# Layer 3 reads its bf16 high part in place; VectorE normalises the next tile ahead of the second row's gated products

## The chip, the cores and the metric

One core of a Trainium2 chip runs the whole kernel as one launch. The metric is the device time of one execution in microseconds; the figure shown is the median of three runs. The engines are PE (TensorE; PEld is its weight load), DVE (VectorE), ACT (ScalarE), POOL (GpSimd) and SP, which issues the DMAs.

## The reference

Four layers work on one image x of 192 by 192 pixels with 64 channels, each as `x = x + L(group_norm(x))`. Cut to what matters, with i, j, k pixel indices and d a channel:

```python
# layers 0, 1, 2
xn = layernorm(v)                               # over the 64 channels, v = group_norm(x)
left, right = (xn@Wl)*sigmoid(xn@Wlg), (xn@Wr)*sigmoid(xn@Wrg)   # times a mask in layers 0 and 1
out = einsum('bikd,bjkd->bijd', left, right)    # layer 2: 'bkjd,bkid->bijd', divided by 192
x = x + (layernorm(out) * sigmoid(xn@Wog)) @ Wout     # layer 1 gates after Wout
# layer 3: no layernorm ahead of the projections
left, right = (v@Wl)*sigmoid(v@Wlg)*mask, (v@Wr)*sigmoid(v@Wrg)*mask
x = x + (layernorm(einsum('bkjd,bkid->bijd', left, right)) @ W_out) * sigmoid(v@W_gate)
```

Layer 0 rounds left and right to bf16 before the einsum; the others are float32.

## The kernel before

The 128 partitions hold 64 channels of two image halves. A tile is two image rows of both halves, 128 by 384 values; each layer has 48 tiles (TILES), and each tile has two rows r = 0, 1, so there are 96 row steps (SUBS) per layer. A layer is three phases in turn: **phase_a** (input normalisation, gate, projections, the products left and right kept in `lr`), **phase_b1** (the einsum, channel by channel) and **phase_b2** (output normalisation, output matmul, residual). The change touches phase_a alone. No planner is at work: every engine has its own queue, written out by hand, and runs strictly in that order; counters (semaphores) hold an instruction until what it needs is there. `over_tiles` calls an engine's `step(n, ...)` for n = 0 to 47, with buffers that rotate by n.

How a tile goes through phase_a of **layers 0, 1 and 2** (`ln` is true):

- PE `centre` (L466) subtracts the channel mean; ACT `centred` copies it out (L715) and squares it (L717); DVE `square_low` (L957) takes the low part of the square; PE `variance` (L474) sums; DVE `var_eps` (L962) copies the variance out; POOL raises it to -1/2 (L1153) and widens it (L1160); PE `spread` (L483) transposes that into PSUM bank 2; DVE `normalise` (L972) multiplies it with the centred tile, which gives `xn`.
- ACT `high` (L748) writes xn + 1 to `val`: float32 in layer 0, and in layers 1 and 2 its bf16 rounding, the high part. There DVE `low` (L978) writes the rest as a second bf16 tile, the low part. Layers 1, 2 and 3 multiply in three passes: high data by high weights, high data by low weights, low data by high weights. Layer 0 has one float32 pass.
- PE `gate` (L493) makes the output gate's argument. PE `project` makes those of one row's left and right: `wide` (L511) 128 of the row's 192 pixels, `narrow` (L521) the other 64. Here the data tile is the weight that is loaded, and the weight matrix streams.
- ACT `sigmoids` (L739) takes one row's gates out of PSUM. DVE `glu` (L989, four instructions for a row, in layers 0, 1 and 3; L996, one instruction, in layer 2) multiplies them with the values in PSUM, writes `lr`, and raises `a_free`: this row's PSUM banks are free.

In **layer 3** there is no layer norm: ACT `plain` (L724) makes xn from the loaded tile, ACT `high` rounds it to bf16, DVE `low` takes the rest. centre, variance, spread, var_eps and normalise don't exist there.

The orders in one step n, which the prediction rests on:

- PE: gate(n), spread(n+1), project(n, 0), project(n, 1), centre(n+4), variance(n+3).
- ACT, layers 0 to 2: gate(n), high(n+1), sigmoids(n, 0), sigmoids(n, 1), centred(n+4). Layer 3: gate(n), high(n+1), plain(n+2), sigmoids(n, 0), sigmoids(n, 1).
- DVE: glu(n-1, 1), var_eps(n+2), normalise(n+1), square_low(n+3), low(n+1), glu(n, 0); in layer 3 only glu(n-1, 1), low(n+1), glu(n, 0).
- SP: the load of a later tile, then the store of gate n to DRAM.

The waits that tie them: `normalise(n+1)` waits for spread(n+1) (`a_bc`), `gate(n)` on PE for low(n) (`a_lo`; layer 0: for high(n)). `project(n, 0)` waits for glu(n-1, 0) ahead of its first pass, and in the layers with a norm ahead of the last pass of `wide` for glu(n-1, 1) as well:

```python
if r == 0 or not ln:
    pe.wait_ge(a_free, l * SUBS + m + 1)         # m = 2n + r; a_free starts at 2
...
if ln and r == 0 and stop:                       # stop: the last of the passes
    pe.wait_ge(a_free, l * SUBS + m + 2)
```

With one pass (layer 0) that is ahead of all of `wide`. In layer 3 project(n, 1) waits for glu(n-1, 1) itself.

Of the kernel before, what the change touches and what calls it, by code (L numbers as in the profile page):

```python
# [20 lines left out]
BF16 = mybir.dt.bfloat16  # L21
U8 = mybir.dt.uint8
ALU = mybir.AluOpType
ACT = mybir.ActivationFunctionType
# [5 lines left out]
ROWS = 2  # L30
# [4 lines left out]
RING = 4  # L35
# [4 lines left out]
SUBS = ROWS * TILES  # L40
# [20 lines left out]
def build_triangle_layers(nc, x_in, params, consts, mask3_k, mask3_row, x_out):  # L61
# [5 lines left out]
    with ExitStack() as ctx:  # L67
        def sb(name, shape, dt=F32):
            return ctx.enter_context(nc.sbuf_tensor(name, shape, dt))

        def sem(name):
            return ctx.enter_context(nc.semaphore(name))

        def sems(name, n=RING):
# [12 lines left out]
        xn = sb("xn", [P, 2, TILE])  # L87
# [33 lines left out]


        sq_high = sq[:, :, :].bitcast(BF16).rearrange("p s (f e) -> p s f e", e=2)[:, :, :, 1]

        xn_parts = val[:, :, :].bitcast(BF16).rearrange("p s (a f) -> p s a f", a=2)

# [28 lines left out]
        a_z, a_cen, a_sq, a_var, a_ve, a_rstd, a_rb, a_bc, a_xn = (  # L155
            sem("a_" + s) for s in ("z", "cen", "sq", "var", "ve", "rstd", "rb", "bc", "xn"))
        a_hi, a_lo, a_sq_lo = sem("a_hi"), sem("a_lo"), sem("a_sq_lo")
        a_gate_mm, a_gate, a_proj, a_sig, a_free = (
            sem("a_" + s) for s in ("gate_mm", "gate", "proj", "sig", "free"))
# [92 lines left out]
        def parts_before(l):  # L252
            return sum(TILES for m in range(l) if IN_PARTS[m])

        def slot_free(eng, semaphore, value):

            if not (isinstance(value, int) and value <= 0):
                eng.wait_ge(semaphore, value)
# [158 lines left out]
        def _(pe):  # L417
# [19 lines left out]
            def phase_a(l):  # L437
                base = l * TILES
                ln = HAS_LN[l]
# [5 lines left out]
                passes = ((0, 0), (1, 0), (0, 1)) if IN_PARTS[l] else ((0, 0),)  # L445

                def moving(part, s):
                    return xn_parts[:, s % 2, part, :] if IN_PARTS[l] else val[:, s % 2, :]

                def half(h):  # L450
# [251 lines left out]
        def _(act):  # L702
            def phase_a(l):
                base = l * TILES
                ln = HAS_LN[l]
                act.wait_ge(gn_dve, 7 * (l + 1))
                act.wait_ge(params_ready, l + 1)

                def centred(n, s):


                    act.wait_ge(a_z, base + n + 1)
                    slot_free(act, a_xn, base + n - RING + 1)
                    slot_free(act, a_var, base + n - 1)
                    nc.scalar.activation(cen[:, s, :], ps[:, s % 2, 0:TILE], ACT.Identity, bias=gn_cb)\  # L715
                        .then_inc(a_cen, 1)
                    nc.scalar.activation(sq[:, s % 2, :], ps[:, s % 2, 0:TILE], ACT.Square, bias=gn_cb)\  # L717
                        .then_inc(a_sq, 1)

                def plain(n, i, s):  # L720

                    act.wait_ge(in_loaded[s], in_count(l) + 16 * (i + 1))
                    slot_free(act, a_lo, parts_before(l) + n - 1)
                    nc.scalar.activation(xn[:, s % 2, :], in_ring[:, s, :], ACT.Identity, bias=gn_b, scale=gn_a)\  # L724
                        .then_inc(a_xn, 1)

                def gate(n, i, s):
                    act.wait_ge(a_gate_mm, base + n + 1)

                    slot_free(act, gate_stored[s], 16 * (l * TURNS + i))  # L730
                    nc.scalar.activation(gate_ring[:, s, :], ps[:, 3, 0:TILE], ACT.Sigmoid, bias=gate_bias[:, 0:1])\  # L731
                        .then_inc(a_gate, 1)

                def sigmoids(n, s, r):
                    m = ROWS * n + r
                    act.wait_ge(a_proj, l * SUBS + m + 1)

                    act.wait_ge(a_free, l * SUBS + m + 1)
                    nc.scalar.activation(act_out[:, r, :].rearrange("p (h c) -> p h c", h=2),  # L739
                                         ps[:, 4 + 2 * r:6 + 2 * r, COLS:2 * COLS], ACT.Sigmoid).then_inc(a_sig, 1)  # L740

                def high(n, s):


                    act.wait_ge(a_xn, base + n + 1)
                    slot_free(act, a_proj, l * SUBS + ROWS * (n - 1))
                    out = xn_parts[:, s % 2, 0, :] if IN_PARTS[l] else val[:, s % 2, :]
                    nc.scalar.activation(out, xn[:, s % 2, :], ACT.Copy, bias=1.0 if ln else 0.0).then_inc(a_hi, 1)  # L748

                def step(n, i, s, ahead):  # L750
                    gate(n, i, s)
                    if not ln and ahead >= 1:
                        high(n + 1, (s + 1) % RING)
                    if not ln and ahead >= 2:
                        plain(n + 2, i + (s + 2) // RING, (s + 2) % RING)
                    if ln and ahead >= 1:
                        high(n + 1, (s + 1) % RING)
                    sigmoids(n, s, 0)
                    sigmoids(n, s, 1)
                    if ln and ahead >= 4:  # L760
                        centred(n + 4, s)

                if ln:
                    centred(0, 0)
                    centred(1, 1)
                    centred(2, 2)
                    centred(3, 3)
                    high(0, 0)
                else:
                    plain(0, 0, 0)  # L770
                    high(0, 0)
                    plain(1, 0, 1)
                over_tiles(act, step)

# [90 lines left out]
        def _(dve):  # L865
# [77 lines left out]
            def phase_a(l):  # L943
                base = l * TILES
                ln = HAS_LN[l]
# [19 lines left out]
                def normalise(n, s):  # L965
                    dve.wait_ge(a_bc, base + n + 1)
                    dve.wait_ge(a_cen, base + n + 1)
                    if IN_PARTS[l]:
                        slot_free(dve, a_lo, parts_before(l) + n - 1)
                    else:  # L970
                        slot_free(dve, a_hi, base + n - 1)
                    nc.vector.tensor_tensor(xn[:, s % 2, :], ps[:, 2, 0:TILE], cen[:, s, :], ALU.mult)\  # L972
                        .then_inc(a_xn, 1)

                def low(n, s):

                    dve.wait_ge(a_hi, base + n + 1)
                    nc.vector.scalar_tensor_tensor(xn_parts[:, s % 2, 1, :], xn[:, s % 2, :], 1.0 if ln else 0.0,  # L978
                                                   xn_parts[:, s % 2, 0, :], ALU.add, ALU.subtract).then_inc(a_lo, 1)

                def glu(n, r):
                    m = ROWS * n + r
                    dve.wait_ge(a_sig, l * SUBS + m + 1)
                    sig = act_out[:, r, :].rearrange("p (h c) -> p h c", h=2)
                    if HAS_MASK[l]:

                        for h in range(2):
                            for t, (lo, hi) in enumerate(((0, P), (P, COLS))):
                                ins = nc.vector.scalar_tensor_tensor(  # L989
                                    out5[:, h, lo // 2:hi // 2, :, m],  # L990
                                    ps[:, 4 + 2 * r + h, lo:hi].rearrange("p (a e) -> p a e", e=2),
                                    mask4[:, t, h, bass.ds(m, 1)],
                                    sig[:, h, lo:hi].rearrange("p (a e) -> p a e", e=2), ALU.mult, ALU.mult)
                        ins.then_inc(a_free, 1)
                    else:
                        nc.vector.tensor_tensor(  # L996
                            out5[:, :, :, :, m],
                            ps[:, 4 + 2 * r:6 + 2 * r, 0:COLS].rearrange("p h (a e) -> p h a e", e=2),
                            sig.rearrange("p h (a e) -> p h a e", e=2), ALU.mult).then_inc(a_free, 1)

                def step(n, i, s, ahead):
                    if not (isinstance(n, int) and n == 0):
                        glu(n - 1, 1)
                    if ln and ahead >= 2:
                        var_eps(n + 2, (s + 2) % RING)
                    if ln and ahead >= 1:
                        normalise(n + 1, (s + 1) % RING)
                    if ln and ahead >= 3:
                        square_low(n + 3, (s + 3) % RING)
                    if IN_PARTS[l] and ahead >= 1:  # L1010
                        low(n + 1, (s + 1) % RING)
                    glu(n, 0)
# [107 lines left out]
            for q in range(PIECES):  # L1120
                dve.wait_ge(x_loaded[q], 16)
                with dve.Fori(q * TURNS // PIECES, (q + 1) * TURNS // PIECES) as i:
                    for s in range(RING):
                        n = i * RING + s
# [183 lines left out]
```

## Time and profile before

| | |
|---|---|
| median of 3 runs | 1529.07 us (1520.78 to 1530.68) |
| profiled execution: its own time, span | 1531.67 us, 1529.5 us |
| busy share of the span: PE, DVE, ACT, POOL | 84%, 68%, 63%, 36% |
| mean granted TensorE clock | 0.948 of full speed |
| busiest DVE group: L989, the gated products | 276.3 us busy, 61.7 us idle before, 55.6 of it until ACT L739 |
| phase_a, first to last tile: layers 0, 1, 2, 3 | 186.7, 172.6, 160.0, 130.7 us |

The shares are averages over twelve phases with different limits, so they do not say what one phase waits for. In a timeline row the bracket names the idle time of that engine just before the row and what ended it. Matmuls are pipelined: the time from one row's start to the next one's start is what the engine spent on it, and the duration reaches to the modelled end of its last result.

### The profile page before, as it was taken

What the parts mean: (1) busy time and instruction counts of PE and PEld (TensorE: products, weight loads), DVE (VectorE), ACT (ScalarE), POOL (GpSimd) and SP (SyncE); (2) the same over time, 40 slices, a digit from 0 to 9 for tenths busy, and PEclk for the clock granted to TensorE, in tenths of its full rate; (3) what the DMA queues carried; (4) which work ended last, traced back from release to release, by engine and by line L of the source; (5) the groups of instructions that cost most, each with busy time, mean ns of one, the idle gap of its engine ahead of it and who ended that gap; (6) DMA issues with size and microseconds to landing.
All of it is one profiled execution on the core that took longest, in us unless ns stands there. A gap on an engine that the chain in (4) does not pass through costs nothing. (4 is left out here: it accounts for less than half of the span.)

```text
span 1529.5 us, 43851 instructions
## 1 busy us (share of the span) xinstructions
PE 1282.1 (84%) x12950; PEld 765.9 (50%) x12950; DVE 1041.8 (68%) x2976; ACT 962.0 (63%) x2093; POOL 543.4 (36%) x490
## 2 busy tenths in 40 slices
PE   0899998787789998989941999999789677799898
PEld 0455554444345455755521666667455333367455
DVE  7577774299789996219950788831499788821587
ACT  0577774489577774129940888831599688822575
POOL 0455551055456563005530666610156200000355
PEclk9899999899899999999975899999899899999999
DMA  8011113467533332896667333359689444369798
GB/s 275 27 52 46 51 51 111 114 202 225 169 101 103 106 115 72 254 286 177 195 152 188 103 115 113 108 174 300 180 262 278 154 141 138 129 185 307 212 291 258
DMA packets 206501, 249.31 MB, mean 163 GB/s; under 512 B 29024, under 2 KB 196320, under 8 KB 206432
## 3 DMA queue, kind: packets, MB, share of 16 engines
q1 hardware_dynamic: 206432, 248.42, 53.1%
q8 instruction: 40, 0.66, 0.2%
q14 instruction: 29, 0.24, 0.0%
HBM read 139.83 MB, written 108.53 MB: 162 GB/s over the span
## 5 line engine op out<-in xcount | busy, mean ns | idle before, releaser
L989 DVE SCALAR_TENSOR_TENSOR lr<-ps,mask,act_out 128x128 f32 (+5 forms) x1152 | 276.3, 310 | 61.7 <-ACT act_out L739 55.6
L1153 POOL TENSOR_TENSOR rstd<-ve,half_col 128x6 f32<-128x6 f32 x144 | 190.2, 1321 | 259.1 <-DVE ve L962 225.4
L511 PE MATMUL ps<-w_parts,val 64*128 64x256 bf16 (+1 forms) x2112 | 222.6, 304 | 47.4 <-DVE lr L989 41.9
L1196 POOL TENSOR_TENSOR new_ring<-val,lr 128x384 f32<-128x384 f32 x96 | 103.4, 1078 | 409.5 <-issue 325.0
L1186 POOL TENSOR_TENSOR val<-act_out,gate_ring 128x384 f32<-128x384 f32 x96 | 118.4, 1233 | 247.2 <-ACT act_out L817 231.1
L739 ACT ACTIVATE act_out<-ps 128x384 f32<-128x384 f32 x384 | 174.9, 481 | 34.2 <-PE ps L511 16.7
L783 ACT ACTIVATE in_ring<-ps 128x768 f32<-128x768 f32 (+1 forms) x64 | 51.8, 810 | 184.0 <-PE ps L579 161.9
L511 PEld LDWEIGHTS ps<-w_parts,val 64*128 64x128 bf16 (+1 forms) x2112 | 90.5, 111 | 133.3 <-DVE lr L989 94.7
L1085 DVE TENSOR_TENSOR sq_low<-sq 128x384 bf16<-128x384 f32 x192 | 120.1, 625 | 52.9 <-ACT sq L796 52.8
L621 PE MATMUL ps<-in_ring,k 128*128 128x384 f32 x288 | 134.5, 555 | 20.1 <-DMA in_ring<-t_scratch 19.7
L715 ACT ACTIVATE cen<-ps,gn 128x384 f32<-128x384 f32 x144 | 83.6, 581 | 104.1 <-PE ps L466 101.5
L794 ACT ACTIVATE cen<-ps 128x384 f32<-128x384 f32 x192 | 104.5, 544 | 66.9 <-PE ps L621 66.4
L748 ACT ACTIVATE val<-xn 128x384 bf16<-128x384 f32 (+1 forms) x192 | 99.9, 521 | 64.1 <-PE ps L521 41.1
L579 PE MATMUL ps<-lr 64*128 64x192 f32 (+3 forms) x896 | 129.2, 335 | 12.8 <-DVE lr L989 5.2
L1036 DVE COPY cen<-ps 128x384 f32<-128x384 f32 x48 | 26.7, 557 | 162.1 <-PE ps L579 158.4
L1160 POOL TENSOR_TENSOR rb<-rstd,one_col 128x384 f32<-128x384 f32 x144 | 129.0, 896 | 11.3
L466 PE MATMUL ps<-in_ring,w_centre 128*128 128x192 f32 (+1 forms) x288 | 93.6, 440 | 44.4 <-issue 44.2
L579 PEld LDWEIGHTS ps<-lr 64*128 64x128 f32 (+3 forms) x896 | 105.5, 181 | 33.6 <-issue 18.4
L809 ACT ACTIVATE rb<-rstd 128x384 f32<-128x384 f32 x192 | 110.4, 575 | 17.6 <-DVE rstd L1046 17.1
L731 ACT ACTIVATE gate_ring<-ps,gate_bias 128x384 f32<-128x384 f32 x192 | 111.5, 581 | 12.6 <-PE ps L493 8.3
L521 PE MATMUL ps<-w_parts,val 64*64 64x128 bf16 (+1 forms) x4224 | 119.0, 234 | 0.0
L957 DVE TENSOR_TENSOR sq_low<-sq 128x384 bf16<-128x384 f32 x144 | 79.8, 554 | 55.6 <-ACT sq L717 55.6
(101 smaller groups left out, 2574.8 us busy)
## 6 DMA issues: line engine op xcount, KB each, us to landing
gate_scratch<-gate_ring SPq DMA_DIRECT2D x192, 192.0 KB, 2.2
gate_ring<-gate_scratch SPq DMA_DIRECT2D x96, 384.0 KB, 3.7
in_ring<-x_scratch SPq DMA_DIRECT2D x144, 192.0 KB, 2.4
lr<-x_scratch SPq DMA_DIRECT2D x72, 384.0 KB, 4.5
in_ring<-t_scratch SPq DMA_DIRECT2D x144, 192.0 KB, 3.3
x_scratch<-new_ring SPq DMA_DIRECT2D x48, 384.0 KB, 2.9
t_scratch<-in_ring SPq DMA_DIRECT2D x48, 384.0 KB, 3.4
lr<-x SPq DMA_DIRECT2D x6, 1536.0 KB, 15.3
```

Of the source, the lines that this page charges most:

```text
L511: mm = nc.tensor.matmul(banks[h][:, :, 0:P], moving(x, s)[half(h), N * r:N * r + P], proj_weights(w, h)[:, 0:2 * P], start=start, stop=sto ...
L521: mm = nc.tensor.matmul(banks[h][TAIL * e:TAIL * e + TAIL, :, P:COLS], moving(x, s)[half(h), N * r + P:N * r + N], proj_weights(w, h)[:, 2 ...
L579: mm = nc.tensor.matmul(ps[:, b + i % 2, N * (i // 2):N * (i // 2) + N], left[:, 0:P], right, start=first and i < 2, stop=last and i >= 2, ...
L621: nc.tensor.matmul(ps[:, s % 2, 0:TILE], w_c, t_slots(l, s)[:, 0, :], start=True, stop=True).then_inc(b2_z, 1)
L731: nc.scalar.activation(gate_ring[:, s, :], ps[:, 3, 0:TILE], ACT.Sigmoid, bias=gate_bias[:, 0:1])\
L739: nc.scalar.activation(act_out[:, r, :].rearrange("p (h c) -> p h c", h=2), ps[:, 4 + 2 * r:6 + 2 * r, COLS:2 * COLS], ACT.Sigmoid).then_i ...
L809: nc.scalar.activation(rb[:, s % 2, :].rearrange("p (a c) -> p a c", c=C), rstd[:, s % 2, :].rearrange("p (a o) -> p a o", o=1) .broadcast ...
L989: ins = nc.vector.scalar_tensor_tensor(out5[:, h, lo // 2:hi // 2, :, m], ps[:, 4 + 2 * r + h, lo:hi].rearrange("p (a e) -> p a e", e=2), ...
L1085: nc.vector.tensor_tensor(sq_low[:, s % 2, :], sq[:, s % 2, :], sq_high[:, s % 2, :], ALU.subtract).then_inc(b2_sq_lo, 1)
L1153: nc.gpsimd.tensor_tensor(rstd[:, s % 2, :], ve[:, s % 2, :], half_col[:, :], ALU.pow)\
L1160: nc.gpsimd.tensor_tensor(rb[:, s % 2, :].rearrange("p (a c) -> p a c", c=C), rstd[:, s % 2, :].rearrange("p (a o) -> p a o", o=1) .broadc ...
L1186: nc.gpsimd.tensor_tensor(val[:, s % 2, :], act_out[:, s % 2, :], gate_ring[:, s, :], ALU.mult)\
```

## The change

`xn_high` is a view of the float32 tile `xn` that takes the upper two bytes of each value: a bf16 number, cut off and not rounded, at every second bf16 position. Layer 3's PE reads it where it read the high part in `val`, ACT's `high` goes in layer 3, and DVE's `low` subtracts the view from xn with another instruction. `low` now waits for xn itself, and for the PE to be done with the tile before last; `plain`, whose tile PE now reads too, waits for PE where it waited for `low`, and stands behind the sigmoids in ACT's step. In layers 0, 1 and 2 DVE's `glu(n-1, 1)` stands behind `var_eps(n+2)` and `normalise(n+1)`, where it stood ahead of them.

```diff
--- before.py
+++ after.py
@@ -122,6 +122,8 @@
 
         sq_high = sq[:, :, :].bitcast(BF16).rearrange("p s (f e) -> p s f e", e=2)[:, :, :, 1]
 
+        xn_high = xn[:, :, :].bitcast(BF16).rearrange("p s (f e) -> p s f e", e=2)[:, :, :, 1]
+
         xn_parts = val[:, :, :].bitcast(BF16).rearrange("p s (a f) -> p s a f", a=2)
 
         w_whole = w_parts[:, :, :].rearrange("p a f -> p (a f)").bitcast(F32)
@@ -445,6 +447,8 @@
                 passes = ((0, 0), (1, 0), (0, 1)) if IN_PARTS[l] else ((0, 0),)
 
                 def moving(part, s):
+                    if not ln and part == 0:
+                        return xn_high[:, s % 2, :]
                     return xn_parts[:, s % 2, part, :] if IN_PARTS[l] else val[:, s % 2, :]
 
                 def half(h):
@@ -720,7 +724,7 @@
                 def plain(n, i, s):
 
                     act.wait_ge(in_loaded[s], in_count(l) + 16 * (i + 1))
-                    slot_free(act, a_lo, parts_before(l) + n - 1)
+                    slot_free(act, a_proj, l * SUBS + ROWS * (n - 1))
                     nc.scalar.activation(xn[:, s % 2, :], in_ring[:, s, :], ACT.Identity, bias=gn_b, scale=gn_a)\
                         .then_inc(a_xn, 1)
 
@@ -745,20 +749,18 @@
                     act.wait_ge(a_xn, base + n + 1)
                     slot_free(act, a_proj, l * SUBS + ROWS * (n - 1))
                     out = xn_parts[:, s % 2, 0, :] if IN_PARTS[l] else val[:, s % 2, :]
-                    nc.scalar.activation(out, xn[:, s % 2, :], ACT.Copy, bias=1.0 if ln else 0.0).then_inc(a_hi, 1)
+                    nc.scalar.activation(out, xn[:, s % 2, :], ACT.Copy, bias=1.0).then_inc(a_hi, 1)
 
                 def step(n, i, s, ahead):
                     gate(n, i, s)
-                    if not ln and ahead >= 1:
-                        high(n + 1, (s + 1) % RING)
-                    if not ln and ahead >= 2:
-                        plain(n + 2, i + (s + 2) // RING, (s + 2) % RING)
                     if ln and ahead >= 1:
                         high(n + 1, (s + 1) % RING)
                     sigmoids(n, s, 0)
                     sigmoids(n, s, 1)
                     if ln and ahead >= 4:
                         centred(n + 4, s)
+                    if not ln and ahead >= 2:
+                        plain(n + 2, i + (s + 2) // RING, (s + 2) % RING)
 
                 if ln:
                     centred(0, 0)
@@ -768,7 +770,6 @@
                     high(0, 0)
                 else:
                     plain(0, 0, 0)
-                    high(0, 0)
                     plain(1, 0, 1)
                 over_tiles(act, step)
 
@@ -974,9 +975,15 @@
 
                 def low(n, s):
 
-                    dve.wait_ge(a_hi, base + n + 1)
-                    nc.vector.scalar_tensor_tensor(xn_parts[:, s % 2, 1, :], xn[:, s % 2, :], 1.0 if ln else 0.0,
-                                                   xn_parts[:, s % 2, 0, :], ALU.add, ALU.subtract).then_inc(a_lo, 1)
+                    if ln:
+                        dve.wait_ge(a_hi, base + n + 1)
+                        nc.vector.scalar_tensor_tensor(xn_parts[:, s % 2, 1, :], xn[:, s % 2, :], 1.0,
+                                                       xn_parts[:, s % 2, 0, :], ALU.add, ALU.subtract).then_inc(a_lo, 1)
+                    else:
+                        dve.wait_ge(a_xn, base + n + 1)
+                        slot_free(dve, a_proj, l * SUBS + ROWS * (n - 1))
+                        nc.vector.tensor_tensor(xn_parts[:, s % 2, 1, :], xn[:, s % 2, :], xn_high[:, s % 2, :],
+                                                ALU.subtract).then_inc(a_lo, 1)
 
                 def glu(n, r):
                     m = ROWS * n + r
@@ -999,12 +1006,12 @@
                             sig.rearrange("p h (a e) -> p h a e", e=2), ALU.mult).then_inc(a_free, 1)
 
                 def step(n, i, s, ahead):
-                    if not (isinstance(n, int) and n == 0):
-                        glu(n - 1, 1)
                     if ln and ahead >= 2:
                         var_eps(n + 2, (s + 2) % RING)
                     if ln and ahead >= 1:
                         normalise(n + 1, (s + 1) % RING)
+                    if not (isinstance(n, int) and n == 0):
+                        glu(n - 1, 1)
                     if ln and ahead >= 3:
                         square_low(n + 3, (s + 3) % RING)
                     if IN_PARTS[l] and ahead >= 1:
```

## Rows read from the trace of the kernel before

**Rows 1.** Windows: start:end, length, busy us of PE, PEld, DVE, ACT, POOL, clock, DMA.

```profile
51.30:238.00 186.70, 183.28 (x1703) 104.31 (x1703) 138.97 (x507) 136.62 (x276) 99.81 (x94) 0.98 0.14 49
...
420.90:593.50 172.60, 155.53 (x2306) 85.59 (x2306) 159.66 (x555) 130.10 (x277) 101.85 (x93) 0.99 0.31 100
...
1207.10:1337.80 130.70, 100.81 (x1776) 47.62 (x1776) 109.16 (x406) 114.23 (x231) 0.00 (x0) 0.98 0.42 136
```

**Rows 2.** One line in layers 0, 1, 2, 3: ns min/median/max, first to last start.

```profile
L972 DVE TENSOR_TENSOR xn<-ps,cen x48: 545/557/558, 51.3 to 238.0; 128x384 f32<-128x384 f32 x48
...
L972 DVE TENSOR_TENSOR xn<-ps,cen x48: 541/545/558, 420.9 to 593.5; 128x384 f32<-128x384 f32 x48
...
L972 DVE TENSOR_TENSOR xn<-ps,cen x48: 556/558/559, 843.1 to 1003.1; 128x384 f32<-128x384 f32 x48
...
L724 ACT ACTIVATE xn<-in_ring,gn x48: 692/695/706, 1207.1 to 1337.8; 128x384 f32<-128x384 f32 x48
```

**Rows 3.** Timeline of layer 0: start, us, engine, line, op, [idle before <-releaser].

```profile
150.85 0.99 DVE L989 SCALAR_TENSOR_TENSOR lr<-ps,mask,act_out 128x128 f32 x4 [0.17 <-issue]
...
151.86 0.56 DVE L972 TENSOR_TENSOR xn<-ps,cen 128x384 f32<-128x384 f32 x1
...
151.90 0.70 PE L511 MATMUL ps<-w_parts,val 64*128 64x256 f32 x4
...
155.39 0.49 PE L483 MATMUL ps<-k,rb 128*128 128x128 f32 x3
...
155.92 0.56 DVE L972 TENSOR_TENSOR xn<-ps,cen 128x384 f32<-128x384 f32 x1 [0.23 <-PE ps L483]
```

**Rows 4.** Timeline of layer 1.

```profile
501.93 0.55 DVE L972 TENSOR_TENSOR xn<-ps,cen 128x384 f32<-128x384 f32 x1
...
502.00 0.28 PE L511 MATMUL ps<-w_parts,val 64*128 64x256 bf16 x2 [0.30 <-DVE lr L989]
...
502.22 0.53 PE L521 MATMUL ps<-w_parts,val 64*64 64x128 bf16 x24
...
502.40 0.55 DVE L957 TENSOR_TENSOR sq_low<-sq 128x384 bf16<-128x384 f32 x1
...
504.50 0.51 PE L483 MATMUL ps<-k,rb 128*128 128x128 f32 x3
```

**Rows 5.** Timeline of layer 2.

```profile
855.16 0.53 PE L521 MATMUL ps<-w_parts,val 64*64 64x128 bf16 x24
...
856.46 1.01 DVE L996 TENSOR_TENSOR lr<-ps,act_out 128x384 f32<-128x384 f32 x2
...
857.45 0.49 PE L483 MATMUL ps<-k,rb 128*128 128x128 f32 x3
```

**Rows 6.** Timeline of layer 3.

```profile
1281.19 0.36 PE L521 MATMUL ps<-w_parts,val 64*64 64x128 bf16 x12
...
1282.20 0.98 ACT L739 ACTIVATE act_out<-ps 128x384 f32<-128x384 f32 x2
...
1282.85 1.89 DVE L989 SCALAR_TENSOR_TENSOR lr<-ps,mask,act_out 128x128 f32 x8 [0.56 <-ACT act_out L739]
...
1283.89 0.50 PE L511 MATMUL ps<-w_parts,val 64*128 64x256 bf16 x6 [0.66 <-DVE lr L989]
...
1284.65 0.55 DVE L978 SCALAR_TENSOR_TENSOR val<-xn,val 128x384 bf16<-128x384 f32 x1
...
1284.76 0.47 ACT L739 ACTIVATE act_out<-ps 128x384 f32<-128x384 f32 x1
```

**Rows 7.** Weight loads of line 474: every second bf16 value (sq), and packed (sq_low).

```profile
L474 PEld LDWEIGHTS ps<-sel_bf,sq x432: 95/97/151, 47.0 to 998.3; 128*128 128x128 bf16 x144
...
L474 PEld LDWEIGHTS ps<-sel_bf,sq_low x432: 94/96/151, 47.0 to 998.4; 128*128 128x128 bf16 x144
```

**Rows 8.** Timeline of layer 0: the gate's products on a slow and a full clock.

```profile
53.12 1.63 PE L493 MATMUL ps<-val,w_gate 128*128 128x384 f32 x2
...
154.66 0.89 PE L493 MATMUL ps<-val,w_gate 128*128 128x384 f32 x2
```

## The prediction, made before the changed kernel ran

> **What bounds the kernel now.** The change is in phase_a, so I read that phase of each layer alone. First the windows: in layer 0 PE is busy 183.28 of 186.70 us; in layer 1 DVE is the busiest, 159.66 of 172.60; in layer 3 no engine is full (ACT 114.23, DVE 109.16, PE 100.81 of 130.70) [rows 1]. Then the pace. 48 instructions of a line have 47 gaps from first start to last, so a tile takes (238.0 - 51.3)/47 = 3.97 us in layer 0, 172.6/47 = 3.67 in layer 1, 160.0/47 = 3.40 in layer 2 and 130.7/47 = 2.78 in layer 3 [rows 2]. Then timelines of single tiles, for what each engine waits for.
>
> In layer 0 the reader should see that DVE runs the second row's products (150.85 to 151.84) while PE is still in `spread`; PE's `wide` starts at 151.90, 0.06 us after them, and DVE's normalise runs at 151.86, beside it [rows 3]. In layer 1 PE stands idle for 0.30 us before the last pass at 502.00, waiting for those products, and again normalise runs beside PE's next work [rows 4]. So today the products are made while PE works on gate and spread, and normalise while PE works on the projections: each hides behind the other engine.
>
> **The change, part by part.** *Layers 0 to 2, the swap.* It adds and removes no instruction. It builds one closed chain. PE's step runs gate(n), spread(n+1), project(n, 0). normalise(n+1) can't start before spread(n+1) has ended. glu(n-1, 1) now stands behind it on DVE. And the last pass of project(n, 0)'s `wide` waits for glu(n-1, 1), with all the rest of PE's step queued behind it: narrow, row 1, centre, variance, the next gate, the next spread. So every tile must now take, one after the other:
>
> - S, PE's work from that last pass to the end of the next spread. Layer 0 (one pass, so from the start of `wide`): 151.90 to 155.39 + 0.49 = 155.88, 3.98 us [rows 3]. Layer 1: 502.00 to 504.50 + 0.51 = 505.01, 3.01 us [rows 4]. Layer 2: from narrow at 855.16 to 857.45 + 0.49 = 857.94 is 2.78 [rows 5], and the last pass ahead of it 0.22 as in layer 1 (502.00 to 502.22) [rows 4]: 3.00.
> - From spread's end to normalise: 155.88 to 155.92, 0.04 [rows 3].
> - normalise until the next DVE instruction can start: 501.93 to 502.40, 0.47 [rows 4].
> - The second row's products: 0.99 for four instructions [rows 3] in layers 0 and 1; in layer 2 half of a pair that takes 1.01 less its overlap [rows 5], for which I take one instruction at normalise's 0.55 [rows 4], the same kind and shape.
> - From their end to PE: 0.06 [rows 3].
>
> Layer 0: 3.98 + 0.04 + 0.47 + 0.99 + 0.06 = 5.54 us a tile, 1.57 more than 3.97. Layer 1: 3.01 + 1.56 = 4.57, 0.90 more. Layer 2: 3.00 + 1.12 = 4.12, 0.72 more. Tiles n = 1 to 46 have both instructions, 46 of them: 72.2 + 41.4 + 33.1 = **146.7 us more**.
>
> Does anything else go round more slowly than this chain, or shorten it? variance needs square_low, which DVE does right behind the products and which takes 0.55 [rows 4], while PE has its projections and centre ahead of variance. gate(n+1) needs `low` (layer 0: `high`), and normalise, its source, is done earlier against PE than now. POOL's two steps start with var_eps, and have a whole longer tile. So the stall changes hands: PE waits some 1.5 us a tile, DVE waits for spread, and glu(n, 0) and the sigmoids have slack.
>
> *Layer 3, `high` goes.* 48 instructions of ACT, 0.51 us each going by their neighbours' pace, leave a queue that isn't full. What counts is the order. Now `high` and `plain` stand ahead of the sigmoids: narrow of row 0 ended at 1281.19 + 0.36 = 1281.55, and its sigmoid began at 1282.20, 0.65 us later, for which DVE then waited 0.56. In the tile after, where ACT was free, it is 0.08: PE starts at 1283.89, the sigmoid at 1284.76 [rows 6]. With the sigmoids straight behind the gate the second case should hold for every tile. Then the chain is: products of row 0 from 1282.85 until PE's project at 1283.89, 1.04; to the sigmoid, 0.87; the sigmoid 0.47; and 0.16 until DVE starts (1282.20 + 0.49, half of 0.98, to 1282.85) [rows 6]. Together 2.54 us, 0.24 under 2.78; with 47 tiles **11.3 us less**. DVE alone would need 1284.65 - 1282.85 + 0.55 = 2.35 [rows 6], which would be 20 us less; if ACT is late in another place, nothing is gained.
>
> *Layer 3, the rest.* `low` becomes a subtraction with a strided bf16 operand. The nearest row is square_low, the same kind and sizes, 0.55 [rows 4], against 0.55 now [rows 6]: nothing. PE's weight loads of the strided view: line 474 loads both kinds, 97 ns strided and 96 packed [rows 7]: nothing. The gate's products stream the view, for which I have no row; below nothing it can't go, since the columns stay, and were it slower, PE's idle 0.66 us ahead of project [rows 6] covers it, and only what goes over that would cost. `plain`, moved behind the sigmoids, has ACT's next gate behind it. It is 0.70 us [rows 2], the time between row 1's sigmoid and the next gate has room for it, and its new wait is met, because the sigmoids ahead of it wait for the same projections. SP's load waits for `plain`, with the store of the gate queued behind; both go some 1.3 us later in a step, while load and gate buffers are four tiles (10 us) deep: nothing. The first `high` of the layer goes, 0.5 us, inside the rounding.
>
> **Sum.** 146.7 - 11.3 = 135.4. The profiled execution took 1531.67 us (span 1529.5), 2.6 above the median, so 1667 for it and **1664 us** beside the median of 1529.07.
>
> **Rivals.** *The filled gap, faster.* In layer 1 DVE is the fullest engine, and before `low` it waits for ACT's `high`, which itself waits for normalise. Normalise first means `high` runs beside the products, and this wait goes: at most the 172.60 - 159.66 = 12.9 us in which DVE idles in layer 1 [rows 1]. With layer 3's 11.3 that is 24 us less, 1505. The Trainium skill, "Perfetto Trace Analysis", Optimization Strategy, says to find the gaps on the engine that one optimises, to see what it waits for, and to let that start sooner; by that rule alone the swap is right. It decides if DVE could do normalise and the products, 0.47 + 0.99, before PE asks for them. Against it: PE already asks 0.30 us too early in layer 1 [rows 4], and in layer 0 spread ends just where `wide` wants to start. Chance 0.04.
>
> *Only layer 3 moves, about the same.* If spread(n+1) had long ended whenever DVE comes to it, the swap would be free, and 11 us less would remain: 1518. The row of normalise waiting 0.23 us for spread [rows 3] speaks against it. Chance 0.03.
>
> *The clock falls, far slower.* PE would idle about 1.5 us in each tile. In layer 3 it idles 30 of 131 us and its granted clock is 0.98 [rows 1]; the new layers 0 to 2 would have PE busy for about 72% (3.98 of 5.54), near layer 3's 77%, so I expect it to stay. If it fell to the lower level in all of them, S would grow as the gate's products do, 1.63 against 0.89 us [rows 8], by 83%: 0.83 x (3.98 + 3.01 + 3.00) x 46 = 381 us, about 2045. The Trainium skill, "TensorE: Matmul & The Clock Gate", Part 1, has the throttled clock as the default state that activity lifts, and names gaps between bursts as what brings it back. Layer 3's row shows gaps of up to 0.66 us without that; no row here has a gap of 1.5. Chance 0.06.
>
> **How the numbers follow.** My chain has 0.87, and 1664 is its time. Upwards: DVE's issue gap of 0.17 [rows 3] in each tile, and normalise at its full 0.56 in place of 0.47, make 0.26 x 138 = 36 us; layer 2's mean of 3.40 lies 0.40 above S, part of it the first two passes, which DVE's work now covers; if all of it came on top, it is 18: 1718. Downwards: layer 3 at DVE's 2.35 (9 us) and no latency at the two handovers (0.10 x 138 = 14): 1641, taken as 1638. The range leaves out the three rivals, 0.13. One per cent is 15 us, about what a measurement of this kernel tells from no change: slower 0.87 + 0.06 = 0.93, same 0.03, faster 0.04.
>
> **What would show it.** normalise's lines should be 5.5, 4.6 and 4.1 us apart; `wide` (L511) in layers 0 to 2 should show a wait of about 1.5, 1.2 and 0.8 us for DVE's products in each tile; normalise should wait for spread (L483) in each; and layer 3's `low` should wait for nothing, at 2.5 us a tile. I am wrong if `wide` doesn't wait longer than now, if the granted clock in layers 0 to 2 falls well under 0.98, or if layer 3 doesn't get shorter.

## The result and the profile after

The changed kernel takes **1688.92 us**, median of 4 runs (1685.32 to 1691.92), against 1527.34 us for the kernel before on the same chip. The ratio is 1.1064, 95% interval 1.1031 to 1.1097: 10.6% slower. The profiled execution took 1689.6 us, with a span of 1687.1 against 1529.5. The forecast of 1664 us had the direction and the place; it was 25 us short.

Line 973 is normalise, as line 972 was, and line 728 is `plain`, as 724 was; one row for each layer, with ns and first to last start, as in [rows 2].

```profile
L973 DVE TENSOR_TENSOR xn<-ps,cen x48: 556/557/558, 54.4 to 331.1; 128x384 f32<-128x384 f32 x48
...
L973 DVE TENSOR_TENSOR xn<-ps,cen x48: 556/558/559, 516.2 to 729.2; 128x384 f32<-128x384 f32 x48
...
L973 DVE TENSOR_TENSOR xn<-ps,cen x48: 556/558/559, 980.7 to 1175.5; 128x384 f32<-128x384 f32 x48
...
L728 ACT ACTIVATE xn<-in_ring,gn x48: 692/697/707, 1377.0 to 1498.2; 128x384 f32<-128x384 f32 x48
```

Over 47 tiles these are 276.7, 213.0, 194.8 and 121.2 us, or 5.89, 4.53, 4.14 and 2.58 us a tile. Against [rows 2] that is +90.0, +40.4, +34.8 and -9.5 us. The four make +155.7 of the span's +157.6, so next to nothing else moved. The windows of the same four stretches (busy us of PE, PEld, DVE, ACT, POOL, then granted clock and DMA), to be read against [rows 1]:

```profile
54.40:331.10 276.70, 205.16 (x1703) 112.11 (x1703) 141.87 (x504) 141.47 (x276) 99.82 (x93) 0.91 0.09 33
...
516.20:729.20 213.00, 153.56 (x2302) 89.14 (x2302) 166.59 (x551) 139.79 (x276) 99.82 (x93) 0.99 0.25 81
...
980.70:1175.50 194.80, 153.63 (x2392) 102.22 (x2394) 144.37 (x277) 139.53 (x276) 100.37 (x94) 0.99 0.27 88
...
1377.00:1498.20 121.20, 102.67 (x1797) 48.50 (x1797) 110.93 (x411) 91.07 (x186) 0.00 (x0) 0.98 0.46 148
```

In layers 0 to 2 no engine is full any more: in layer 0 PE is busy 205.16 of 276.7 us where it was 183.28 of 186.7. The tiles show why. The timeline of the changed kernel, a layer 0 tile, a layer 1 tile and the last pass of one in layer 2:

```profile
159.27 0.70 PE L515 MATMUL ps<-w_parts,val 64*128 64x256 f32 x4 [1.55 <-DVE lr L996]
...
162.76 0.49 PE L487 MATMUL ps<-k,rb 128*128 128x128 f32 x3
...
163.29 0.56 DVE L973 TENSOR_TENSOR xn<-ps,cen 128x384 f32<-128x384 f32 x1 [0.92 <-PE ps L487]
...
163.76 0.98 DVE L996 SCALAR_TENSOR_TENSOR lr<-ps,mask,act_out 128x128 f32 x4
...
164.80 0.49 PE L515 MATMUL ps<-w_parts,val 64*128 64x256 f32 x2 [1.55 <-DVE lr L996]
...
565.28 0.56 DVE L973 TENSOR_TENSOR xn<-ps,cen 128x384 f32<-128x384 f32 x1 [0.75 <-PE ps L487]
...
566.79 0.28 PE L515 MATMUL ps<-w_parts,val 64*128 64x256 bf16 x2 [1.32 <-DVE lr L996]
...
1056.59 0.28 PE L515 MATMUL ps<-w_parts,val 64*128 64x256 bf16 x2 [0.88 <-DVE lr L1003]
```

Read it as one chain. In layer 0 the spread ends at 162.76 + 0.49 = 163.25, normalise starts at 163.29, the second row's products at 163.76, they end at 164.74, and PE's `wide` starts at 164.80 after 1.55 us of idle time that DVE's products end. In [rows 3] normalise and `wide` started side by side, at 151.86 and 151.90. From `wide` to `wide` it is 5.53 us, where the prediction summed 5.54. Layer 1 shows the same with 1.32 us of idle time, layer 2 with 0.88. Over the three layers normalise waited for spread in 48, 46 and 48 of its 48 instructions.

### The profile page after: what moved, and what is told of

The parts are those of the page before. It is cut to its first block and busy times, and to the rows that moved or that the text cites. A ratio compares the mean times of both kernels' runs of the same rounds, so it can differ in the third digit from the quotient of the medians.

```text
span 1687.1 us, 43792 instructions
## 1 busy us (share of the span) xinstructions
PE 1301.2 (77%) x12950; PEld 774.8 (46%) x12950; DVE 1064.7 (63%) x2976; ACT 960.8 (57%) x2045; POOL 535.0 (32%) x490
## 5 line engine op out<-in xcount | busy, mean ns | idle before, releaser
L515 PE MATMUL ps<-w_parts,val 64*128 64x256 bf16 (+1 forms) x1728 | 212.4, 316 | 172.3 <-DVE lr L996 131.8
L996 DVE SCALAR_TENSOR_TENSOR lr<-ps,mask,act_out 128x128 f32 (+5 forms) x1152 | 285.2, 310 | 93.0 <-ACT act_out L743 89.0
L743 ACT ACTIVATE act_out<-ps 128x384 f32<-128x384 f32 x384 | 188.1, 490 | 201.5 <-PE ps L525 170.2
L515 PEld LDWEIGHTS ps<-w_parts,val 64*128 64x128 bf16 (+1 forms) x1728 | 80.3, 116 | 247.0 <-DVE lr L996 157.8
L973 DVE TENSOR_TENSOR xn<-ps,cen 128x384 f32<-128x384 f32 x144 | 80.3, 557 | 125.8 <-PE ps L487 125.7
L719 ACT ACTIVATE cen<-ps,gn 128x384 f32<-128x384 f32 x144 | 83.6, 581 | 131.0 <-PE ps L470 130.7
L1092 DVE TENSOR_TENSOR sq_low<-sq 128x384 bf16<-128x384 f32 x192 | 119.0, 620 | 53.7 <-ACT sq L797 53.6
L958 DVE TENSOR_TENSOR sq_low<-sq 128x384 bf16<-128x384 f32 x144 | 109.1, 758 | 56.9 <-ACT sq L721 56.9
L470 PE MATMUL ps<-in_ring,w_centre 128*128 128x192 f32 (+1 forms) x288 | 90.9, 429 | 45.8 <-issue 45.5
L1167 POOL TENSOR_TENSOR rb<-rstd,one_col 128x384 f32<-128x384 f32 x144 | 119.8, 832 | 11.3
L642 PE MATMUL ps<-k,rb 128*128 128x128 f32 x576 | 100.1, 283 | 13.5 <-ACT rb L810 11.9
```

Of the source, the lines that this page charges most:

```text
L515: mm = nc.tensor.matmul(banks[h][:, :, 0:P], moving(x, s)[half(h), N * r:N * r + P], proj_weights(w, h)[:, 0:2 * P], start=start, stop=sto ...
L958: nc.vector.tensor_tensor(sq_low[:, s % 2, :], sq[:, s % 2, :], sq_high[:, s % 2, :], ALU.subtract).then_inc(a_sq_lo, 1)
L996: ins = nc.vector.scalar_tensor_tensor(out5[:, h, lo // 2:hi // 2, :, m], ps[:, 4 + 2 * r + h, lo:hi].rearrange("p (a e) -> p a e", e=2), ...
L1092: nc.vector.tensor_tensor(sq_low[:, s % 2, :], sq[:, s % 2, :], sq_high[:, s % 2, :], ALU.subtract).then_inc(b2_sq_lo, 1)
L1167: nc.gpsimd.tensor_tensor(rb[:, s % 2, :].rearrange("p (a c) -> p a c", c=C), rstd[:, s % 2, :].rearrange("p (a o) -> p a o", o=1) .broadc ...
```

## The experiments

Ratios are to the kernel before, timed on the same chip; the tile times are from each kernel's own trace.

**swap_only.** The kernel before with nothing but DVE's new order:

```diff
 def step(n, i, s, ahead):          # DVE, phase_a
-    if not (isinstance(n, int) and n == 0):
-        glu(n - 1, 1)
     if ln and ahead >= 2:
         var_eps(n + 2, (s + 2) % RING)
     if ln and ahead >= 1:
         normalise(n + 1, (s + 1) % RING)
+    if not (isinstance(n, int) and n == 0):
+        glu(n - 1, 1)
```

Expected: 

> The kernel before with the swap alone; layer 3 as before. Theory (closed chain spread, normalise, products, last pass of wide): layers 0, 1 and 2 take as long as in the changed kernel, 90 + 40 + 35 us more than before by the first and last normalise of each, so about 1692 us. Rival (a good part of the loss comes with layer 3's part, or from both together): under 1620.

Measured: 1694.84 us, ratio 1.1104 (1.1063 to 1.1145). Normalise in layers 0 to 2, and `plain` in layer 3:

```profile
L972 DVE TENSOR_TENSOR xn<-ps,cen x48: 557/558/559, 54.5 to 329.6; 128x384 f32<-128x384 f32 x48
...
L972 DVE TENSOR_TENSOR xn<-ps,cen x48: 557/558/559, 513.1 to 726.2; 128x384 f32<-128x384 f32 x48
...
L972 DVE TENSOR_TENSOR xn<-ps,cen x48: 557/558/559, 979.6 to 1174.0; 128x384 f32<-128x384 f32 x48
...
L724 ACT ACTIVATE xn<-in_ring,gn x48: 692/696/706, 1374.1 to 1505.4; 128x384 f32<-128x384 f32 x48
```

275.1, 213.1 and 194.4 us as in the changed kernel, and layer 3 at 131.3 as before. The swap alone makes the whole loss.

**l3_only.** The other half: the changed kernel with DVE's old order in layers 0 to 2 (the diff above, the other way round).

Expected: 

> The changed kernel with DVE's old order in layers 0 to 2, so layer 3's part alone. Theory: layer 3's tile at 2.58 us as in the changed kernel against 2.78, some 9.5 us off, so about 1517 us. Rival (the strided reads cost PE what ACT saves, and the changed kernel's layer 3 is short for another reason): 1527.

Measured: 1516.69 us, ratio 0.9934 (0.9911 to 0.9958): 0.7% faster, about what layer 3 gains. `plain` in layer 3:

```profile
L728 ACT ACTIVATE xn<-in_ring,gn x48: 692/697/706, 1203.4 to 1325.1; 128x384 f32<-128x384 f32 x48
```

121.7 us in place of 130.7. Layer 3's part is sound, and the strided reads cost nothing that shows. The seven kernels of this document that have this part whole take 121.2 to 122.0 us in layer 3, the two without it 130.7 and 131.3.

**wait_row1.** Does PE's wait make the loss, or DVE's order as such? The order stays new, but PE waits where it needs the banks:

```diff
-if r == 0 or not ln:
-    pe.wait_ge(a_free, l * SUBS + m + 1)
+pe.wait_ge(a_free, l * SUBS + m + 1)
...
-if ln and r == 0 and stop:
-    pe.wait_ge(a_free, l * SUBS + m + 2)
...
-if r == 0 or not ln:
-    wide()
-    mm = narrow()
-else:
-    narrow()
-    mm = wide()
+wide()
+mm = narrow()
```

Expected: 

> The changed kernel, but PE waits for the second row's products where it needs their banks, ahead of row 1's projections (which go wide, then narrow), and no longer in row 0. Theory: row 0's last pass and narrow, 1.23 us in layer 0 (152.15 to 153.38 in the changed kernel) and 0.68 in layers 1 and 2, leave the chain and run under the stall: tiles of 4.30, 3.85 and 3.47 us, so 0.58 x 46 = 27 us over the kernel before less 9.5 of layer 3, about 1544. Rival (DVE's new order is slow by itself, whatever PE waits for): about 1689 still.

Measured: 1590.27 us, ratio 1.0437 (1.04 to 1.0474). Normalise in layers 0, 1, 2:

```profile
L965 DVE TENSOR_TENSOR xn<-ps,cen x48: 557/557/558, 53.5 to 269.6; 128x384 f32<-128x384 f32 x48
...
L965 DVE TENSOR_TENSOR xn<-ps,cen x48: 557/558/559, 452.8 to 648.5; 128x384 f32<-128x384 f32 x48
...
L965 DVE TENSOR_TENSOR xn<-ps,cen x48: 557/558/558, 896.6 to 1074.6; 128x384 f32<-128x384 f32 x48
```

That is 4.60, 4.16 and 3.79 us a tile. 99 us of the loss come back by moving PE's wait alone (layer 0's clock, below, among them: it is 1.00 here), so most of the loss isn't DVE's order by itself. The forecast of 1544 was 46 us too low, and had a slip: the stretch from 152.15 to 153.38 holds the narrow products of both rows (16 instructions in one row of the timeline), and only row 0's leave the chain. Recounted after the run, that is 0.63 + half of 0.60 = 0.93 in layer 0, and 5.53 - 0.93 = 4.60 is what was measured. In layers 1 and 2 the last pass (0.21) and half of narrow's 0.46 make 0.44, which gives 4.53 - 0.44 = 4.09 and 3.70, against 4.16 and 3.79.

**filled_l0.** Layer 0 was 0.35 us a tile above the sum, though a clean tile fits it to 0.01. In the timeline of the changed kernel, centre (L470) in a slow tile and in a clean one:

```profile
154.44 1.65 PE L470 MATMUL ps<-lr,w_centre 128*128 x2
...
161.13 0.91 PE L470 MATMUL ps<-lr,w_centre 128*128 x2
```

And the windows around them (the clock is the third number from the end):

```profile
154.00:156.00 2.00, 2.00 (x9) 0.78 (x6) 0.98 (x4) 0.49 (x1) 0.00 (x0) 0.50 0.00 0
...
160.00:162.00 2.00, 2.00 (x27) 1.14 (x28) 0.92 (x4) 0.98 (x2) 0.00 (x0) 1.00 0.00 0
```

In the slow tile the granted clock is 0.50, the lower of its two levels, and centre takes 1.65 us in place of 0.91. Over all of layer 0 the clock is 0.91; in the kernel before it was 0.98. Tile by tile, 14 of the 47 steps from one normalise to the next take 7.12 us, and nearly all others 5.5. To test whether the idle PE brings this on, PE gets work in the stall:

```diff
+if l == 0 and r == 0:              # in project, once row 0's banks are free
+    for _ in range(6):
+        nc.tensor.matmul(ps[:, 4, 384:512], k_centre, k[:, 0:128], start=True, stop=True)
```

Expected: 

> The changed kernel; in layer 0 PE does six matmuls of 128x128 into unused columns of a bank of row 0 during the stall, once that bank is free; their results are not used. Theory (layer 0's 5.89 us a tile instead of 5.54 is the granted clock, which falls in some tiles after the 1.55 us of waiting): granted clock in layer 0 at 0.98 or more, 5.55 us a tile, so 16 us less, about 1673. Rival (layer 0's chain is longer than I summed, clock aside): 5.9 us a tile or more, 1689 or above.

Measured: 1664.99 us, ratio 1.0913 (1.0881 to 1.0944), 24 us less than the changed kernel. Its window of layer 0, and rows of one tile and the next (the six matmuls, L508, stand there as twelve records):

```profile
54.10:311.40 257.30, 246.58 (x2257) 168.58 (x2258) 142.08 (x503) 139.97 (x276) 99.43 (x93) 1.00 0.10 35
```

```profile
158.51 0.98 DVE L999 SCALAR_TENSOR_TENSOR lr<-ps,mask,act_out 128x128 f32 x4
...
159.55 0.70 PE L518 MATMUL ps<-w_parts,val 64*128 64x256 f32 x4 [0.21 <-DVE lr L999]
...
163.37 1.50 PE L508 MATMUL ps<-k 128*128 128x128 f32 x12
```

The clock is 1.00, no step takes 7.12 us any more, and the layer takes 257.3 us or 5.47 a tile: 19.4 us less than in the changed kernel, and 70.6 over the kernel before. PE still starts `wide` 0.06 us after DVE's products (159.49 to 159.55): the chain is untouched, only the clock has changed. So layer 0's excess was the clock, and it falls because PE stands idle in the stall. With 1.32 and 0.88 us of waiting, layers 1 and 2 keep 0.99; what makes the difference between 1.55 and 1.32 no run here shows, since the layers' matmuls differ too.

**var_first.** Of the two instructions that went ahead of the products, only var_eps stays there:

```diff
 if ln and ahead >= 2:
     var_eps(n + 2, (s + 2) % RING)
-if ln and ahead >= 1:
-    normalise(n + 1, (s + 1) % RING)
 if not (isinstance(n, int) and n == 0):
     glu(n - 1, 1)
+if ln and ahead >= 1:
+    normalise(n + 1, (s + 1) % RING)
```

Expected: 

> The changed kernel with only var_eps ahead of the second row's products and normalise behind them again. Theory (normalise carries the chain, because it waits for spread in the same PE step; var_eps waits for the variance of the PE step before): at most 0.1 us a tile over the kernel with layer 3's part alone, so 1517 to 1530 us. Rival (anything ahead of the products makes PE late, also an instruction that waits for the step before): over 1600.

Measured: 1536.51 us, ratio 1.0053 (1.0036 to 1.007), 6.5 us above the forecast's end. DVE's new order costs 172 us (1688.92 against l3_only's 1516.69); normalise carries 152 of them, but var_eps, with the other 20, isn't free. A layer 0 tile and a piece of a layer 1 tile:

```profile
149.99 0.16 DVE L963 TENSOR_SCALAR ve<-ps 128x6 f32<-128x6 f32 x1
...
150.23 0.99 DVE L996 SCALAR_TENSOR_TENSOR lr<-ps,mask,act_out 128x128 f32 x4
...
151.28 0.70 PE L515 MATMUL ps<-w_parts,val 64*128 64x256 f32 x4 [0.24 <-DVE lr L996]
...
502.75 1.05 POOL L1167 TENSOR_TENSOR rb<-rstd,one_col 128x384 f32<-128x384 f32 x1
...
503.33 0.89 DVE L980 SCALAR_TENSOR_TENSOR val<-xn,val 128x384 bf16<-128x384 f32 x1 [0.21 <-ACT val L752]
```

In layer 0 the products start 0.24 us behind var_eps's own start, and `wide` waits 0.24 us for them; in 14 of the tiles var_eps has waited for PE's variance before. It is a short chain of the same kind, 198.9 us for the layer against 185.7 in l3_only. Layer 1 takes 184.2 against 171.5: POOL's widening (L1167) now runs beside `low`, which takes 0.89 us in place of 0.55 on the engine that was busiest there. That this is all of layer 1's loss is not shown.

**spread_early.** The new order with the closing link taken out: PE makes the spread a step earlier.

```diff
 gate(n, s)
-if ln and ahead >= 1:
-    spread(n + 1, (s + 1) % RING)
 project(n, s, 0)
 project(n, s, 1)
+if ln and ahead >= 2:
+    spread(n + 2, (s + 2) % RING)
...
 variance(2, 2)
+spread(1, 1)                       # ahead of the loop
```

Expected: 

> The changed kernel with DVE's new order, but PE makes the spread one step earlier, behind row 1's projections and ahead of centre. Theory: the closed chain is gone, and another one closes: var_eps to POOL's power 0.31, its widening 1.40, 0.83, 0.06 to spread, 0.44, centre 0.75, variance 0.29, 0.05 to the next var_eps, 4.13 us a tile in each of layers 0 to 2; so (0.16 + 0.46 + 0.73) x 46 = 62 us over 1517, about 1579. Rival (DVE's new order is slow by itself): 1650 or more.

Measured: 1605.7 us, ratio 1.0489 (1.0459 to 1.0518), 27 us above the forecast and well under the rival. A tile takes 4.85, 4.18 and 3.91 us in layers 0, 1 and 2, where 4.13 was expected in each. In layer 0:

```profile
153.69 0.55 PE L487 MATMUL ps<-k,rb 128*128 128x128 f32 x3
...
155.14 0.16 DVE L964 TENSOR_SCALAR ve<-ps 128x6 f32<-128x6 f32 x1 [0.51 <-PE ps L478]
...
155.34 0.56 DVE L974 TENSOR_TENSOR xn<-ps,cen 128x384 f32<-128x384 f32 x1
...
155.82 0.98 DVE L997 SCALAR_TENSOR_TENSOR lr<-ps,mask,act_out 128x128 f32 x4
...
156.85 0.70 PE L515 MATMUL ps<-w_parts,val 64*128 64x256 f32 x4 [1.09 <-DVE lr L997]
```

spread (L487) is done long before normalise, so the old chain is gone. But DVE comes to normalise only behind var_eps, which waited 0.51 us for the variance (L478); then normalise, the products, and `wide` at 156.85, 1.09 us late. My sum had left out that var_eps now stands ahead of the products too. Nor does layer 1 bear the sum out, near as it comes:

```profile
465.10:661.70 196.60, 153.38 (x2302) 83.84 (x2302) 187.29 (x550) 134.37 (x275) 112.73 (x94) 0.99 0.27 87
```

DVE is busy 187.29 of 196.60 us, with a median of 1.19 us for `low` beside POOL's widening, so that layer is full on DVE; and layer 2's 3.91 is under what the chain was to take at the least.

**l3_plain_last.** What in layer 3 makes its gain? The kernel before, with only the order changed:

```diff
 def step(n, i, s, ahead):          # ACT, phase_a
-    if not ln and ahead >= 2:
-        plain(n + 2, i + (s + 2) // RING, (s + 2) % RING)
...
     if ln and ahead >= 4:
         centred(n + 4, s)
+    if not ln and ahead >= 2:
+        plain(n + 2, i + (s + 2) // RING, (s + 2) % RING)
```

Expected: 

> The kernel before with one edit in layer 3: ACT makes the next xn (plain) behind the sigmoids; the rounding to bf16 (high) stays. Theory (layer 3 gains because nothing holds the sigmoids up): with high's 0.41 us still ahead of them some of it comes, 2.62 to 2.68 us a tile, 5 to 8 us off, 1518 to 1521. Rival (the gain is ACT's saved work): 2.78, 1526.

Measured: 1521.01 us, ratio 0.9959 (0.9938 to 0.998), at the upper end of what the theory gave. But its trace doesn't bear it out:

```profile
L724 ACT ACTIVATE xn<-in_ring,gn x48: 693/697/709, 1199.9 to 1328.1; 128x384 f32<-128x384 f32 x48
```

128.2 us, 2.73 a tile: 2.5 us off layer 3, a quarter of the 9, where I had expected 2.62 to 2.68. The order alone is the smaller part. The waits point to what holds it: over layer 3 DVE's products wait 2.1 us for the sigmoids where they waited 14.7, but `low` now waits 12.1 us for ACT's `high` (3.8 before) and PE's gate 6.4 us for `low` (2.4 before). In the changed kernel, without `high`, `low` waits 0.8 us in all. The other 4.2 of the 6.7 us by which the median fell aren't in layer 3 and stay open: layer 3 starts 7.2 us earlier in this trace than in that of the kernel before (1199.9 against 1207.1), behind code that is the same in both.

**l3_plain_first.** The opposite cut: `high` gone, but `plain` ahead of the sigmoids as it was.

```diff
 gate(n, i, s)
+if not ln and ahead >= 2:
+    plain(n + 2, i + (s + 2) // RING, (s + 2) % RING)
...
-if not ln and ahead >= 2:          # behind the sigmoids
-    plain(n + 2, i + (s + 2) // RING, (s + 2) % RING)
```

Expected: 

> Layer 3's part with DVE's old order in layers 0 to 2, but ACT makes the next xn (plain) ahead of the sigmoids, where it stood; the rounding (high) is gone. Theory (layer 3's gain is that high is gone from ACT's queue, the order matters little): 2.58 to 2.62 us a tile in layer 3, 1517 to 1519. Rival (what counts is how much work stands ahead of the sigmoids: 1.01 us gave 2.78, high's 0.41 gave 2.73, none 2.58; plain's 0.60 is between the first two): 2.75, 1525.

Measured: 1613.5 us, ratio 1.0566 (1.0526 to 1.0605). Neither theory had this. The timeline, and the window of layer 3:

```profile
1303.06 0.71 ACT L728 ACTIVATE xn<-in_ring,gn 128x384 f32<-128x384 f32 x1 [2.18 <-PE ps L525]
...
1303.67 0.85 ACT L743 ACTIVATE act_out<-ps 128x384 f32<-128x384 f32 x2
...
1305.36 0.61 PE L515 MATMUL ps<-w_parts,xn 64*128 64x256 bf16 x4 [1.28 <-DVE lr L996]
```

```profile
1211.00:1425.50 214.50, 149.90 (x1795) 61.55 (x1796) 108.22 (x407) 90.22 (x184) 0.00 (x0) 0.61 0.26 83
```

`plain` waits 2.18 us for PE's narrow products (L525), and both sigmoids are queued behind it. Read in place, xn stays in use until PE has done both rows' projections of its tile, so `plain` of the second tile ahead must wait for projections whose sigmoids would come after it. The move behind the sigmoids is thus needed by reading in place. PE's clock falls to 0.61 on top. How the gain divides between order and saved work this run can't tell; only the waits of l3_plain_last speak to it.

**l3_wait_row1.** A try for a better kernel: l3_only with wait_row1's edit.

Expected: 

> Layer 3's part with DVE's old order, and PE's wait for the second row's products moved to row 1 (which goes wide, then narrow). Theory: with the old order only layer 1 has a stall there, 0.30 us of PE, while DVE is the fullest engine, so little moves: 1510 to 1517 us. Rival (PE's stall is layer 1's limit): 0.30 x 46 = 14 us off, 1503.

Measured: 1514.65 us, ratio 0.992 (0.989 to 0.995), which overlaps l3_only's interval. The stall at row 0's last pass cost nothing that shows. Both are under 1% faster than the kernel before, and so faster than either kernel of the case.

## Why the prediction was right, and where it fell short

- **The closed chain** (spread, normalise, products, last pass): shown by swap_only, which has all of the loss, and by wait_row1, spread_early and var_first, which give back 99, 83 and 152 us by changing one link each.
- **Its size.** Forecast +72.2, +41.4 and +33.1 us for layers 0, 1 and 2; measured +90.0, +40.4 and +34.8. Layers 1 and 2 fit to 1.7 us. Most of their tiles take 4.62 and 4.19 us, a little over the 4.57 and 4.12 of the sums, and the first few are shorter, so part of that fit is two small errors that cancel. With the clock at 1.00 (filled_l0) layer 0 takes 70.6 us more than before, against 72.2 forecast.
- **The mis-sized term is layer 0's S**, taken as 3.98 us in every tile. The step that failed is "so I expect it to stay", on the clock, argued from PE's busy share (72% against layer 3's 77%). The clock fell part of the time, to 0.91 in the mean: 14 of 47 tiles took 7.12 us in place of 5.54, some 22 us. So the prediction's own sign of being wrong, a granted clock in layers 0 to 2 well under 0.98, came true in layer 0. The argument from the busy share doesn't hold: layers 0 and 1 came out at 74 and 72%, and only layer 0 lost clock. I had made an all-or-nothing rival of that. The Trainium skill ("TensorE: Matmul & The Clock Gate", Part 1, "A second HAM failure mode") has frequent short idling between groups of matmuls bring the throttle back. This trace agrees, with 0.50 granted in the tile at 154 us.
- **The range held in part by luck.** 1688.92 lies inside 1638 to 1718, but the 25 us above 1664 came mostly from the clock (17.8 in layer 0), which the range had left out as a rival. The room that it took had been made for DVE's issue gaps, a longer normalise and layer 2's first passes, and layers 1 and 2, 0.7 us over their sums together, hardly used it.
- **Layer 3**: forecast -11.3, measured -9.5 us, 2.58 a tile against 2.54. The chain of the sum is there:

```profile
1430.60 0.99 DVE L996 SCALAR_TENSOR_TENSOR lr<-ps,mask,act_out 128x128 f32 x4
...
1430.94 0.52 PE L497 MATMUL ps<-xn,w_gate_parts 128*128 128x384 bf16 x2
...
1431.29 0.33 PE L497 MATMUL ps<-val,w_gate_parts 128*128 128x384 bf16 x1
...
1431.65 0.39 PE L515 MATMUL ps<-w_parts,xn 64*128 64x256 bf16 x4
...
1432.51 0.49 ACT L743 ACTIVATE act_out<-ps 128x384 f32<-128x384 f32 x1
...
1433.17 0.99 DVE L996 SCALAR_TENSOR_TENSOR lr<-ps,mask,act_out 128x128 f32 x4
```

From products to products 2.57 us, with the sigmoid 0.86 behind PE's start. The sum's 0.87 for that was read from a tile "where ACT was free". It wasn't free; this row of the kernel before stands just ahead of that sigmoid (1284.76):

```profile
1284.16 0.70 ACT L724 ACTIVATE xn<-in_ring,gn 128x384 f32<-128x384 f32 x1
```

The sigmoid follows `plain` after 0.60 us, just as in the tile before it (1281.60 to 1282.20), so it came straight behind `plain`, and the row could not show the term by itself. That the 0.87 fits is luck. The gate's two passes over the strided view take 0.35 us (1430.94 to 1431.29), in which PE isn't waited for. What the forecast gave as the cause, the sigmoids' place behind `high` and `plain`, is shown only in part: moving `plain` alone gave 2.5 of 9 us, and the waits of l3_plain_last point to `high` itself, for which `low` waits, as the rest.

- **The rivals.** The filled gap (1505) and layer 3 alone (1518) are out: normalise waits for spread in all tiles but two, as counted above. The clock rival came true in layer 0 alone, at an eighth of its price there: 17.8 us (90.0 - 72.2) of 0.83 x 3.98 x 46 = 152.

## What to carry over

Before an instruction is moved ahead on one engine, follow both of its ends: what it waits for, and who waits for what is now queued behind it. If both are in the same step of the same other in-order engine, the loop is closed and the tile costs the sum, however idle both engines look. And when such a stall lands on TensorE, give its clock a term of its own, with part of the tiles at the lower level as one of the cases: here it was 14 of 47, and a busy share near that of a phase that kept its clock was no ground for setting the term to nothing.

## What was not expected of the hardware

- PE's granted clock fell in single tiles with 1.55 us of waiting per 5.5 us tile (mean 0.91), stayed at 0.99 with 1.32 per 4.5, was 1.00 again with the wait filled, and in l3_plain_first, with waits of 1.28 to 1.75 in the tiles around 1300 us, fell to 0.61.
- When `square_low` or `low` on DVE overlaps POOL's widening, the one that starts second takes longer. In layer 2 of the changed kernel square_low's median is 1058 ns, against 548 in layer 0, where hardly anything overlaps it; here POOL's widening starts first and keeps its 0.83:

```profile
L958 DVE TENSOR_TENSOR sq_low<-sq x48: 547/1058/1192, 976.1 to 1169.6; 128x384 bf16<-128x384 f32 x48
```

```profile
1056.31 0.83 POOL L1167 TENSOR_TENSOR rb<-rstd,one_col 128x384 f32<-128x384 f32 x1
...
1056.45 1.10 DVE L958 TENSOR_TENSOR sq_low<-sq 128x384 bf16<-128x384 f32 x1
```

In layer 0 of var_first it is the other way round, square_low keeps its 0.55 us and the widening takes 1.20:

```profile
151.60 0.55 DVE L958 TENSOR_TENSOR sq_low<-sq 128x384 bf16<-128x384 f32 x1
...
151.64 1.20 POOL L1167 TENSOR_TENSOR rb<-rstd,one_col 128x384 f32<-128x384 f32 x1
```

POOL's power step doesn't do this: in layer 0 of the kernel before it overlaps square_low by some 0.6 us in nearly every tile, and square_low stays at 0.55. `low` behaves the same way: in the kernel before it keeps 0.56 us beside a widening of 1.17 where it starts first (21 times), and takes 1.09 beside one of 0.83 where it starts second (24 times). In layer 2 of the changed kernel PE waited for square_low in two tiles at most, so it had slack there; in var_first the longer `low` lay on layer 1's busiest engine.
